# Graph network kernel: when TensorE takes the tiles of a plain sum pass

## The reference

```
L0: msg = sum_s basis_s * (h @ W_s)[src]      (two spline layers, 4 corners each)
L1: out = segment_sum(norm * h[src], dst)     (one plain sum)
L2: msg = relu(h[row] W1a + h[col] W1b + e W1c + b1), then segment_sum(msg, col)
L3: agg = segment_sum(cat(h[dst], h[src], e) @ W.T + b, dst)   (three layers)
```

## Time and profile before

| | us |
|---|---|
| median of three runs | 18001.43 |
| lowest and highest | 17969.0 and 18039.48 |
| the profiled execution's own time | 18151.96 |
| its span | 18150.2 |
| mean granted TensorE clock | 0.607 |
| POOL busy | 11761.6 |
| PE matmul busy | 7905.4 |
| DVE busy | 4686.6 |

### The profile page before, as it was taken

One profiled execution on the slowest core, in us unless ns is written; L12 is line 12 of the kernel. 1 busy time (PEld: TensorE's weight loads), 2 busy tenths in 40 slices (PEclk: granted clock), 3 DMA queues, 4 the chain that ended last, 5 costly groups with the idle time before them and its releaser, 6 DMA issues.

```text
span 18150.2 us, 140082 instructions
## 1 busy us (share of the span) xinstructions
PE 7905.4 (44%) x34014; PEld 6861.4 (38%) x34014; DVE 4686.6 (26%) x7726; ACT 1208.3 (7%) x3388; POOL 11761.6 (65%) x11663
## 2 busy tenths in 40 slices
PE   4365666444443333334545543433324333233334
PEld 3244444333333333334444433333323333233334
DVE  6243433334332111112333321111211111211111
ACT  4011111000000000001111100000000000000000
POOL 0766665777776666656666656666566666566666
PEclk9677777677666555557777765555555555555555
DMA  8355554333332111113333321111111111111111
GB/s 323 104 157 159 157 158 145 98 103 103 104 101 53 29 32 32 32 39 98 100 99 99 100 58 25 26 26 26 22 30 26 26 26 26 26 26 27 27 27 26
DMA packets 901495, 1315.78 MB, mean 72 GB/s; under 512 B 434733, under 2 KB 592718, under 8 KB 875806
## 3 DMA queue, kind: packets, MB, share of 16 engines
q0 software_dynamic: 426240, 764.57, 17.4%
q1 hardware_dynamic: 272702, 372.81, 5.9%
q10 hardware_dynamic: 202464, 177.49, 3.3%
HBM read 966.27 MB, written 347.67 MB: 72 GB/s over the span
## 4 chain that ended last, share of the span: by engine, by line
another core or an unknown queue 54%; issue 16%; PE 14%; DVE 8%; POOL 4%; ACTq 1%; DVEq 1%; DMA 1%; ACT 1%; SPq 0%; POOLq 0%
PE PS L776 9%; POOL BIG L613 4%; DVE OH L1408 2%; PE PS L696 2%; DVE BIG L1421 2%; PE PS L809 2%; PE PS L770 1%; DVE BIG L1428 1%; PE PS L705 1%; ACTq L984 0%; DVE BIG L1436 0%; ACTq L985 0%; DMA AG<-acc 0%; PE PS L681 0%
## 5 line engine op out<-in xcount | busy, mean ns | idle before, releaser
L613 POOL DMA_INDIRECT BIG<-t_mp,IDX x4995 | 4920.5, 985 | 2575.7 <-issue 1780.9
L776 PE MATMUL PS<-BIG,OH 128*128 128x64 f32 (+3 forms) x23310 | 5629.7, 424 | 1372.3 <-DVE BIG L1421 631.9
L776 PEld LDWEIGHTS PS<-BIG,OH 128*128 128x128 f32 x23310 | 5021.9, 294 | 1861.3 <-issue 1205.8
L613 POOL DMA_INDIRECT BIG<-t_cell,IDX x3330 | 3580.6, 1075 | 2019.5 <-issue 1545.4
L770 PE MATMUL PS<-STG,CARRY 128*128 128x64 f32 (+3 forms) x1554 | 557.2, 457 | 6867.4 <-issue 3001.7
L1408 DVE TENSOR_TENSOR OH<-REL,IOTA 128x640 f32<-128x640 f32 x2331 | 1908.3, 822 | 4970.8 <-remote 4134.0
L770 PEld LDWEIGHTS PS<-STG,CARRY 128*128 128x128 f32 x1554 | 355.8, 284 | 7037.5 <-issue 3916.4
L613 POOL DMA_INDIRECT BIG<-t_p,IDX x1665 | 1642.7, 987 | 933.3 <-issue 519.4
L613 POOL DMA_INDIRECT BIG<-t_gcn,IDX x1665 | 1616.6, 971 | 825.3 <-issue 529.2
L1406 DVE TENSOR_SCALAR CARRY<-IOTA,DELTA 128x128 f32<-128x128 f32 x777 | 230.3, 296 | 3647.0 <-remote 2995.6
L1421 DVE TENSOR_TENSOR BIG<-BIG,COEF 128x1280 f32<-128x1280 f32 x666 | 990.5, 1487 | 401.0 <-DMA BIG<-t_cell,IDX 395.8
(11 more groups left out here) (153 smaller groups left out, 3724.2 us busy)
## 6 DMA issues: line engine op xcount, KB each, us to landing
t_cell<-BIG SPq DMA_DIRECT2D x198, 1280.0 KB, 4.5
BIG<-in_dst_row ACTq DMA_DIRECT2D x333, 240.0 KB
BIG<-t_mp,IDX POOLq DMA_INDIRECT x4995
BIG<-t_cell,IDX POOLq DMA_INDIRECT x3330
BIG<-t_gcn,IDX POOLq DMA_INDIRECT x1665
BIG<-in_ef ACTq DMA_DIRECT2D x333, 80.0 KB
BIG<-t_p,IDX POOLq DMA_INDIRECT x1665
BIG<-t_q ACTq DMA_DIRECT2D x333, 48.0 KB
```

Source lines behind the costliest of these rows:

```text
L613: nc.gpsimd.indirect_dma_start(to[:, j, :], None, table, bass.IndirectOffsetOnAxis(ap=IDX[:, at, column:column + 1], axis=0)).then_inc(gat ...
L776: last = nc.tensor.matmul(WIN[:, 0:out_w], OH[:, s % CHUNKS, j * P:(j + 1) * P], src[:, j, :], start=False, stop=(s % CHUNKS == CHUNKS - 1 ...
```

## The change

In the plain sum passes PE's body is replaced by `group_body`. At the first two slots of a group it does nothing. At the third it waits for the third one-hot and for the three gathers of the group, does the carry, and then sums all three chunks. `sum_chunk` is the same, with its count of `chunk_done` at the end of each chunk. The node steps keep their slots. The spline passes and the mlp pass keep their bodies.

```diff
--- before.py
+++ after.py
@@ -790,6 +790,16 @@
                         carry(g)
                     sum_chunk(s)
 
+                def group_body(u, s, first, last):
+                    c, g = s % CHUNKS, u * UNIT + s // CHUNKS
+                    if c == CHUNKS - 1:
+                        pe.wait_ge(oh_ready, cb + u * SLOTS + s + 1)
+                        for q in range(s - c, s + 1):
+                            pe.wait_ge(gathered[q], 16 * CT * (ub + u + 1))
+                        carry(g)
+                        for q in range(s - c, s + 1):
+                            sum_chunk(q)
+
                 def sum_hidden(u, s):
 
                     pe.wait_ge(hid_ready, u * SLOTS + s + 1)
@@ -822,7 +832,7 @@
                     edged_units(pe, mlp_body, node)
                     sum_hidden(z.units - 1, SLOTS - 1)
                 else:
-                    all_units(pe, body, node)
+                    all_units(pe, group_body if kind == "sum" else body, node)
                 tail_steps(node)
 
             def slow_pass(n):
```

## The result

The kernel after takes 18295.68 us (median of three runs, 18224.74 to 18337.2), the one before 18001.43 us. The ratio is 1.0171, with a 95% interval of 1.0149 to 1.0193: 294 us slower, 2.0 us for each of the 148 units. My forecast was 18041 us, no change; the result lies inside the range (17920 to 18530), and the case that happened is the slower rival, which had 0.26 of the chances: 294 us of the 529 us that lie between 18001 and its 18530.

What follows compares the result with a forecast made beforehand. No engine is saturated; it took a gather backlog worked off at 1.44 us each to pace the sum passes. Pass ends 18 + stalls 22 = 40 us on 18152.0, scaled to 18041 us; range 17920 to 18530.

Steps and rivals of the forecast that it cites:

- no change: Whole kernel: the change does hardly what it says, 18001 us; with the neighbouring forecast 0.64, range 17930 to 18090.
- the slower rival: Sum passes: POOL gets one chunk per release, a short cycle more per unit, 494 us, 18530 us; chance 0.26.
- what lies over the second group's delay: Mid-pass: PE's 21.88 us idle before its third group covers the second group's 6 us, so zero from the delays.
- the 22 I charged: Steady part of sum passes: counts leave three together, POOL stalls oftener and shorter, 0.15 us a unit, 22 us.
- The delay itself: Second group of a unit, now behind the node products: ends at 14041.4 in place of 14035.4, 6 us later.
- The lateness taken as given: Mid-pass node step: transposes end 1.28 us after the first group, gap to products 0.57 us, products 3.64 us.
- The backlog: Sum passes: gathers build up a backlog at 1.25 us each, worked off at 1.44 us, PE's counts stuck in it.
- other 8.7 us: A unit of 45 gathers takes 64.8 us, gathers alone 56.2 us; the other 8.7 us are stalls.
- a short cycle of late counts: Trace, 13284.27 to 13294.83: five gathers in 10.56 us where the usual pace gives 7.2, 3.3 us a unit.
- The end of a pass: After the last gathers nothing covers PE: it ends at 15619.6, not 15615.1; 4.5 us, four times, 18 us.
- The removed waits: PE's pairs of waits per chunk: worth nothing, as chunks already follow at 0.2134 us a record without a gap.
- The clock: Grant 0.50, a third burst changes nothing visible; by the skill's rule 22 us gained at pass ends, not 18 lost.

Runs made afterwards that it cites:

- the chain moved: Kernel after with PE's node products moved from slot 3 to 5 and DVE's take from slot 4 to 5, groups whole: 18116.72 us, ratio 1.0072.
- free gathers: Kernel before, sum-pass gathers not waiting for PE, fixed index columns, ones multiplied for gathered rows: 16135.16, 16106.07 and, where before took 18179.07, 20831.26 us.

## Why the prediction failed where it did

The likeliest case was no change, 18041 us. The step that failed is the one on what lies over the second group's delay: "The 6 us fit into that. ... So in the steady part I take zero". It measured 267 us in the sum passes, not the 22 I charged.

- *The delay itself* came out in size: 6 us a unit was worked out for the second group, and where PE is the bound the grouping costs 5.0 us a unit (742 / 148).
- *The lateness taken as given.* The prediction carried the timing of the counts over from the trace of before. It moved the node products ahead of chunk 3 with a gap of 0.57 us between transposes and products, read off the end of a pass. For the kernel before that was no bad reading in mid-pass either: UT is copied a median of 0.8 us after the transposes in acc4 to acc6. But it holds where the transposes come just behind a pause of POOL, and after the change they mostly didn't. In acc4 and acc5 of the kernel after the same copy is a median of 35.8 and 37.8 us late, so the second group is held back not by 6 us but, in the unit shown, by 45.8 us from the end of the transposes (14067.74 to 14113.52). PE's idle 21.88 us couldn't cover that. In acc6, where the median stayed at 2.2 us, the pass lost 4 us and the prediction's chain held. Now and then the count is late in the kernel before too (up to 34.2 us), but there chunk 3 has been summed ahead of it.
- *The backlog*. I read the equal passes as a backlog "worked off at 1.44 us each", and I named its test: that the pace moves at all. It moved, to 1.51 and 1.53 us in acc4 and acc5 (2521.5 / 1665 and 2552.2 / 1665), to 1.29 where counts are prompt, and to 1.38 with no waits. Why it was the same in four passes of before is argued, not shown: POOL pauses as long as PE needs for its counts, so the pauses adjust themselves, and the equal sums of long and short stalls fit that as well as a backlog. The "other 8.7 us" of a unit were not all stalls either: the stalls are 7.06 us, and the rest is gathers longer than the median (891.61 / 902 = 0.99 us on average).
- *The slower rival* had the place and the sign: POOL standing while PE computes. Its price, 3.3 us in each of 148 units (494 us), was too high because only two passes of four fell into it, at 3.4 and 4.2 us a unit (124 / 37 and 154 / 37); that the two come near the price is luck, for the price was read off a short cycle of late counts, and not off the node step's chain. acc6 kept prompt transposes' counts; why it did isn't shown. With only the second group whole it was acc4 that lost most (2465.6 us against 2416.5 and 2420.2, with the UT copy a median of 26.7, 13.9 and 1.1 us late), with the chain moved acc6 (2456.0), so it isn't a property of the pass.
- *The end of a pass*: 4.5 us predicted, four times; measured 4.9, 13.3, 2.9 and 4.4 us, and 7.2 us in the set with prompt counts. The sum of 26 us stands against 18. In acc5 the chain at the end is as I had it (carry to last burst 15785.24 - 15776.50 = 8.7 us), but its start is set by late counts: the products begin at 15770.64, after the last gather.
- *The removed waits* were put at nothing; no run measured them alone. *Instructions* are unchanged but for the waits: the counts on the page are equal.
- *The clock*: two stretches of the kernel after as the earlier trace rows, POOL's gathers alone with the granted clock.

```profile
5906.00:7206.00 1300.00, 900.72 (x905) 0.50 0.16 31
13846.00:15146.00 1300.00, 823.27 (x837) 0.50 0.13 24
```

With three bursts of 30 records a unit the grant stays at 0.50, the 1.2 GHz level, and the bursts take 6.61 us as before, in mid-pass and at the end of acc5. The Trainium skill, in Perfetto Trace Analysis, section Matmul Optimizations, says that power follows utilization and matmuls should run back to back in batches; the 22 us that my estimate made of it at the pass ends did not come, and this trace shows nothing gained by the larger batches. The second row also shows the loss itself: 837 gathers in 1300 us where before 902 were the earlier trace rows.

What stays open: why the counts are late in some sets and not in others (nothing in the program differs; the later sets ran on four different chips, once each, so chip and moment aren't told apart), and whether what is late is the count or the start of the engine that waits. Why the change moved POOL's pauses in acc4 and acc5 and hardly in acc6 is open too, and so is whether the gathers' bytes or their number set the lateness. No version that computes the same sums beat the kernel before.

## What to carry to other kernels

A step's latency read in a trace belongs to the place where the step stood. Here the same copy came 0.8 us after its matmuls when it stood just behind a pause of GpSimd, and over 30 us after them when it stood 20 us further on. So where some counts in a trace are late and others prompt, find out what the prompt ones have in common before a change moves them, and price a chain from engine to engine at the late value as well. Grouping work behind one wait makes its first part wait for the last part's inputs; before doing so, list what stands ahead of that last input on its engine (here the take of the node products on DVE), and leave that one group by chunk. A pace that is equal in several stages is no proof of a fixed limit; it may be, though this wasn't shown here, an engine that pauses just as long as the others need.

## What was not expected of the hardware

- The same program takes 16.1 ms in some sets of runs (16115.32 and 16136.21 us) and 18.0 to 18.2 ms in others (17985.72, 18001.43, 18179.07 us). In the first, POOL's waits for PE sum to 0.3 us in the kernel after.
- In the second, steps between engines are slow while POOL issues indirect gathers (up to 110.55 us of DVE idle and 122.2 us of ACT's with gathers back to back), and prompt when it stops and shortly after it resumes (within 12 us of that, 88 of 89 UT copies came within 3.1 us of their transposes). POOL's waits are then not waste but the time in which the others move: without them 20831 us in place of 18179.
- A change is worth different amounts in the two kinds of set: the grouping 1.0171 on the one, by POOL's stalls, and 1.0084 on the other, by longer gathers (118.7 us beside those of free gathers) and later pass ends (29 us).
